# Low rank products of 64 rows in groups of four, first loads in single rows, and later first weight sums in a two-stage LoRA kernel

## The chip, the cores and the metric

The kernel runs on one core of one Trainium2 chip. The metric is the time of one execution on the device in microseconds (us). Lower is better.

## The reference

There are 8 batch elements of 512 tokens and 2048 features, all in 32-bit floats. Two linear layers follow each other, each with its input added. The first picks one of 8 full weights per batch element. The second has one weight, a bias, and a low rank part of rank 16 picked per batch element:

```python
w = weight[adapter_ids]                      # L0: 8 x (2048, 2048)
x = x + jnp.einsum('bsi,boi->bso', x, w)
base_out = jnp.einsum('bti,oi->bto', x, W) + b
lora_h = jnp.einsum('bti,bir->btr', x, A)    # A = lora_As[adapter_mapping]
lora_out = jnp.einsum('btr,bro->bto', lora_h, Bm)
x = x + base_out + lora_out * 2.0
```

## The kernel before

Every product runs on TensorE as 128 x 128 weights against 128 rows by 512 tokens, and each operand is split into a high part (rounded to TensorE's 32-bit format, by ScalarE) and a low part (the rest, a subtraction on VectorE or GpSimd). A full product is then three: high times high, high times low, low times high (L856 to L858 in stage 1).

**Stage 1** (to about 1460 us) computes x1 = x + first layer. It runs over 8 batch elements and 16 output tiles each (128 tiles n). A tile has 16 rows k of 128 inputs, so 48 products, into one of two banks `sums`. VectorE adds x to it (L777) and splits it, and `add_h` (L845, L846) multiplies x1 by A of the low rank part into `h_sum`. `a_mix` holds A four times beside itself (high and low), so that the 128 rows of `h_mix` are four groups of 32; `b_mix` holds B of rank 16 eight times, the last 64 rows as low part. h and B go to DRAM (`hs`, `bs`) for stage 2. In between, VectorE forms sums of blocks of the second weight (`sum_q`, 28 units of four steps, one step per tile), which GpSimd stores (`store_q`).

**The start.** SyncE issues the loads of x (8 pieces `x_first` of 2 rows, 512 KB) and of the first two tiles' weights (8 pieces `W_FIRST` of 4 rows, 256 KB) in a written order. ScalarE (`x_hi_part`, `w_hi_part`) and VectorE (`x_lo_part`, `w_lo_part`) split them in the same order. TensorE does 14 products with zeros meanwhile (L867), then the first two tiles alternately by piece.

**Stage 2** computes the second layer by two nested levels of a fast block scheme: 98 steps s, that is 14 outer (`o` = 0 to 6, twice) with 7 inner ones (`j` = 0 to 6). A step has four tiles m of 12 products (L914). Steps j = 0, 2, 4, 5 write `bank_x`, the others `bank_y`, four banks each. VectorE adds each finished tile to one or two sums in SBUF (L822, L824, `acc_free`), splits the next step's x (`xc_lo`, L751, behind tiles 0 and 1), and forms the one after (`add_terms`, L737 to L744, behind tile 3). Weights come through `wl` (5 buffers), split by ScalarE (L593) and GpSimd (L429).

**Low rank products** (L929). 32 of the 98 steps (table `LOW_RANK`, j = 0, 4 or 5, all with products in `bank_x`) carry four of them. Behind each tile m, one product of 128 rows, `bm` (B) against `hm` (h), goes into `bank_y[m]`, which is idle in such a step. VectorE adds it with the bias behind the additions of the same tile (`add_low_rank`, L701). The next step that writes `bank_y` (j = 1 or 6) waits per tile for that addition, in the line

```python
if j in (1, 6) and before is not None:
    pe.wait_ge(low_rank_added, before + m + 1)
```

SyncE loads `bm` (7 buffers, one per product, L329), each behind the wait for an old product.

Of the kernel before, what the change touches and what calls it, by code (L numbers as in the profile page):

```python
# [5 lines left out]
P = 128  # L6
F32 = mybir.dt.float32
# [64 lines left out]
def build(nc, xT, ids0, ids1, w0T, w1T, bias, lora_a, lora_b, yT):  # L72
# [4 lines left out]
    PARTS = 2  # L77
    NG = P // (2 * R)
    TILES = NB * NT
# [5 lines left out]
    WL = 5  # L85
# [4 lines left out]
    WARM = 14  # L90
# [8 lines left out]
    bs = scratch("bs", (NB, 2, P, HALF * P))  # L99
# [31 lines left out]
    with ExitStack() as ctx:  # L131
# [60 lines left out]
        w_first = [[sem(f"w_first{n}_{part}") for part in range(2 * PARTS)] for n in range(2)]  # L192
# [4 lines left out]
        x_first = [sem(f"x_first{c}") for c in range(XC)]  # L197
# [46 lines left out]
        W_FIRST = [(0, 0), (1, 0), (0, 1), (1, 1), (0, 2), (0, 3), (1, 2), (1, 3)]  # L244

        def w_parts(n):

            return 2 * PARTS if n < 2 else PARTS

        def w_ks(n, part):  # L250
            size = KT // w_parts(n)
            return slice(part * size, (part + 1) * size)

        def w_count(n, part):

            if n < 2:
                return W_FIRST.index((n, part)) + 1
            return len(W_FIRST) + (n - 2) * PARTS + part + 1

        def w_done(n):  # L260

            return w_count(n, w_parts(n) - 1)
# [34 lines left out]
        def _(sp):  # L297
            def load_x_first(c):
                sp.dma_start(x_raw[:, x_rows(0, c)], xT[0, c]).then_inc(x_first[c], 16)  # L299
# [3 lines left out]
            for c in range(2):  # L303
                load_x_first(c)
            sp.wait_ge(ids0_loaded, 16)
            for b in range(NB):
                adapter = sp.value_load(ids_sb[0:1, 0, b:b + 1], min_val=0, max_val=ADAPTERS - 1)
                for t in range(NT):
                    n = b * NT + t
                    s = n % 2  # L310
                    for i, (first_n, part) in enumerate(W_FIRST if n == 0 else ()):
                        ks = w_ks(first_n, part)
                        sp.dma_start(w_raw[first_n][:, ks], w0T[bass.ds(adapter, 1), first_n, :, ks]  # L313
                                     .rearrange("a p k o -> (a p) k o")).then_inc(w_first[first_n][part], 16)
                        for c in ((), (2,), (3,), (), (4, 5), (6, 7), (), ())[i]:
                            load_x_first(c)
                    if n >= 2:
                        sp.wait_ge(w_ready, w_done(n - 2))
                        for part in range(PARTS):
                            ks = w_ks(n, part)  # L320
# [6 lines left out]
            def load_bm(i):  # L327
                b, o = low_rank_place(i)[0:2]
                sp.dma_start(bm[i % BM][:].bitcast(F32), bs[b, o // HALF, :, o % HALF * P:(o % HALF + 1) * P]  # L329
                             ).then_inc(bm_loaded[i % BM], 16)  # L330
# [8 lines left out]
            for s in range(SEQ):  # L339
                for m in range(Q):  # L340
# [4 lines left out]
                    if n == 2 * WL:  # L345
                        sp.wait_ge(b_stored, NB * 2 * 16)
# [23 lines left out]
        def _(pool):  # L370
# [8 lines left out]
            def load_b(b, half):  # L379
                if 2 * b + half > 0:  # L380
                    pool.wait_ge(b_ready, 2 * b + half)
# [51 lines left out]
            pool.wait_ge(x_first[XC - 2], 16)  # L433
# [4 lines left out]
            for b in range(NB):  # L438
                for t in range(NT):
# [26 lines left out]
                    if t == 3 and b < NB - 1:  # L466
                        pool.wait_ge(a_ready, (b + 1) * NG)
# [3 lines left out]
                    if n < UNITS * 4:  # L471
                        u, step = divmod(n, 4)
# [19 lines left out]
            for n in range(3, SEQ * Q + 13):  # L492
# [13 lines left out]
                if n == 17:  # L506

                    pool.wait_ge(h_stored, NB * 16)
                    pool.wait_ge(b_stored, NB * 2 * 16)
# [29 lines left out]
        def _(act):  # L539
            def w_hi_part(n, part):  # L540
# [421 lines left out]
```

## Time and profile before

| | us |
|---|---|
| median of 3 runs | 2564.01 |
| lowest, highest | 2562.82, 3201.55 |
| profiled execution | 2562.13 |
| its span | 2560.6 |
| TensorE busy | 2553.9 |
| VectorE busy | 1666.0 |
| GpSimd busy | 1251.4 |
| ScalarE busy | 875.7 |

Spans and rows are in us from the start of the span of the profiled execution. PE is TensorE, DVE VectorE, ACT ScalarE, POOL GpSimd, SP SyncE; a q behind the name is the engine's queue that issues transfers. A product is drawn with its whole way through the array, so that neighbours overlap; the pace is read from start to start. "Idle before" names who ended the idle time ahead of an instruction.

### The profile page before, as it was taken

The numbers are of one execution on the slowest core, as the hardware profiler recorded it, in microseconds if no ns is written. First come the engines' busy times: TensorE is split into PE (matmuls) and PEld (weight loads), VectorE is DVE, ScalarE is ACT, GpSimd is POOL, SyncE is SP. The second block draws the span as 40 slices with busy tenths as digits, with TensorE's granted clock in tenths as the row PEclk, the third lists the DMA queues.
The fourth block names the chain that finished last, engine by engine and source line by source line (L and its number), as shares of the span: only waits on it lengthen the run. The fifth ranks groups of instructions, "written<-read, shape, count | busy, mean of one in ns | idle before, by whom it ended". The sixth has DMA issues, their size and how long they took to land.

```text
span 2560.6 us, 31029 instructions
## 1 busy us (share of the span) xinstructions
PE 2553.9 (100%) x11246; PEld 2112.2 (82%) x11246; DVE 1666.0 (65%) x1885; ACT 875.7 (34%) x1161; POOL 1251.4 (49%) x1471
## 2 busy tenths in 40 slices
PE   9999999999999999999999999999999999999999
PEld 7888888888888888888888888888888888888887
DVE  5445455454354454364443368999998689999995
ACT  4232232232232232232322234343343343333333
POOL 3434434443454334334323466556666655556655
PEclk9999999999999999999999999999999999999999
DMA  9998888998999887899977887457777855546764
GB/s 340 330 302 295 299 285 282 299 285 281 272 297 336 269 290 273 261 292 284 295 190 196 223 310 265 139 173 251 266 240 254 292 168 175 155 150 203 238 224 143
DMA packets 238939, 648.03 MB, mean 253 GB/s; under 512 B 30148, under 2 KB 46532, under 8 KB 238788
## 3 DMA queue, kind: packets, MB, share of 16 engines
q0 software_dynamic: 123440, 393.28, 48.2%
q1 hardware_dynamic: 115060, 252.24, 30.6%
q8 instruction: 90, 1.47, 0.2%
q14 instruction: 61, 0.50, 0.1%
q10 hardware_dynamic: 288, 0.52, 0.1%
HBM read 433.07 MB, written 212.86 MB: 252 GB/s over the span
## 4 chain that ended last, share of the span: by engine, by line
PE 98%; DMA 1%; SPq 0%; DVE 0%; issue 0%; POOL 0%; POOLq 0%; DVEq 0%
PE bank L914 42%; PE bank L856 18%; PE bank L857 18%; PE bank L858 18%; PE bank L845 1%; PE bank L929 1%; PE bank L846 1%; DMA q_raw<-w1T 1%; DMA ids_sb<-ids 0%; SPq L299 0%; SPq L313 0%; DVE q_raw L712 0%; DVE w_lo L667 0%; POOL q_raw L402 0%; POOLq L375 0%
## 5 line engine op out<-in xcount | busy, mean ns | idle before, releaser
L914 PE MATMUL bank<-xc,wl 128*128 128x512 f32 x4704 | 1087.6, 389 | 0.1
L914 PEld LDWEIGHTS bank<-xc,wl 128*128 128x128 f32 x4704 | 882.9, 188 | 183.7 <-issue 0.5
L856 PE MATMUL bank<-x_hi,w_hi 128*128 128x512 f32 x2048 | 797.1, 389 | 0.9 <-DVE w_lo L667 0.9
L429 POOL TENSOR_TENSOR wl<-wl 128x512 fp32r<-128x512 f32 x392 | 599.5, 1548 | 406.0 <-ACT wl L593 404.4
L857 PE MATMUL bank<-x_lo,w_hi 128*128 128x512 f32 x2048 | 796.8, 389 | 0.0
L858 PE MATMUL bank<-x_hi,w_lo 128*128 128x512 f32 x2048 | 796.7, 389 | 0.0
L547 ACT ACTIVATE w_hi<-w_raw 128x1024 fp32r<-128x1024 f32 (+1 forms) x260 | 258.4, 1039 | 969.5 <-PE bank L858 964.4
L777 DVE TENSOR_TENSOR x_raw<-bank,x_raw 128x512 f32<-128x512 f32 x128 | 88.5, 691 | 693.5 <-PE bank L858 634.5
L856 PEld LDWEIGHTS bank<-x_hi,w_hi 128*128 128x128 f32 x2048 | 384.4, 188 | 82.1 <-DVE w_lo L667 2.0
L858 PEld LDWEIGHTS bank<-x_hi,w_lo 128*128 128x128 f32 x2048 | 384.4, 188 | 79.9
L857 PEld LDWEIGHTS bank<-x_lo,w_hi 128*128 128x128 f32 x2048 | 384.4, 188 | 79.7
L446 POOL DMA_DIRECT2D x1s<-x_raw x128 | 70.1, 548 | 656.1 <-DVE x_raw L777 656.1
L822 DVE TENSOR_TENSOR c<-bank,c 128x512 f32<-128x512 f32 x448 | 295.6, 681 | 102.2 <-PE bank L914 98.7
L593 ACT ACTIVATE wl<-wl 128x512 fp32r<-128x512 f32 x392 | 240.5, 624 | 349.5 <-DMA wl<-w1s 332.8
L751 DVE TENSOR_TENSOR xc<-xq,xc 128x1024 fp32r<-128x1024 f32 x196 | 335.9, 1714 | 5.2 <-ACT xc L604 5.1
L667 DVE TENSOR_TENSOR w_lo<-w_raw,w_hi 128x1024 fp32r<-128x1024 f32 (+1 forms) x260 | 302.6, 1204 | 48.4 <-ACT w_hi L547 48.4
L604 ACT ACTIVATE xc<-xq 128x1024 fp32r<-128x1024 f32 x196 | 206.4, 1054 | 314.9 <-DVE xq L741 133.7
L409 POOL DMA_DIRECT2D w1s<-q_raw x196 | 108.7, 574 | 150.4 <-DVE q_raw L712 62.5
L824 DVE TENSOR_TENSOR c<-c,bank 128x512 f32<-128x512 f32 x224 | 146.6, 676 | 15.9 <-PE bank L914 15.9
L701 DVE SCALAR_TENSOR_TENSOR c<-bank,bias_sb,c 128x512 f32<-128x512 f32 x128 | 96.1, 751 | 4.5
L782 DVE TENSOR_TENSOR x_lo<-x_raw,x_hi 128x512 fp32r<-128x512 f32 x128 | 87.4, 683 | 1.5 <-ACT x_hi L584 1.5
L584 ACT ACTIVATE x_hi<-x_raw 128x512 fp32r<-128x512 f32 x128 | 78.7, 615 | 26.6 <-PE bank L858 17.7
(44 smaller groups left out, 1262.8 us busy)
## 6 DMA issues: line engine op xcount, KB each, us to landing
w_raw<-w0T SPq DMA_DIRECT2D x252, 512.0 KB, 7.7
wl<-w1s SPq DMA_DIRECT2D x392, 256.0 KB, 2.9
xss<-x_raw POOLq DMA_DIRECT2D x256, 256.0 KB, 4.5
w1s<-q_raw POOLq DMA_DIRECT2D x196, 256.0 KB, 7.3
q_raw<-w1T POOLq DMA_DIRECT2D x96, 512.0 KB, 9.8
xq<-xss POOLq DMA_DIRECT2D x40, 1024.0 KB, 6.9
x1s<-x_raw POOLq DMA_DIRECT2D x128, 256.0 KB, 2.9
c<-x1s POOLq DMA_DIRECT2D x32, 1024.0 KB, 7.0
```

The lines of the kernel that those rows point to most:

```text
L429: pool.tensor_tensor(w[:, 1], w[:, 1].bitcast(F32), w[:, 0].bitcast(F32), ALU.subtract).then_inc(wl_ready, 1)
L547: act.activation(w_hi[s][:, ks], w_raw[s][:, ks], ACT.Copy).then_inc(w_hi_done, 1)
L593: act.activation(wl[n % WL][:, 0], wl[n % WL][:, 1].bitcast(F32), ACT.Copy).then_inc(wl_hi_done, 1)
L604: act.activation(xc[s % 2][:, 0, ks], xq[place][:, ks], ACT.Copy).then_inc(xc_hi_done, 1)
L667: dve.tensor_tensor(w_lo[s][:, ks], w_raw[s][:, ks], w_hi[s][:, ks].bitcast(F32), ALU.subtract).then_inc(w_ready, 1)
L751: dve.tensor_tensor(xc[s % 2][:, 1, ks], xq[PLACE[s % INNER]][:, ks], xc[s % 2][:, 0, ks].bitcast(F32), ALU.subtract).then_inc(xc_ready, 1)
L822: op = dve.tensor_tensor(tile, bank[m][:], tile, ALU.add)
L824: op = dve.tensor_tensor(tile, tile, bank[m][:], ALU.subtract)
L856: pe.matmul(sums[s][:], w_hi[s][:, k, :], x_hi[:, k, :], start=(k == 0), stop=False)
L857: pe.matmul(sums[s][:], w_hi[s][:, k, :], x_lo[:, k, :], start=False, stop=False)
L858: mm = pe.matmul(sums[s][:], w_lo[s][:, k, :], x_hi[:, k, :], start=False, stop=(k == KT - 1))
L914: mm = pe.matmul(bank[m][:], w[:, w_part, k, :], x[:, x_part, k, :], start=(p == 0 and k == 0 and BEGIN[j]), stop=(p == 2 and k == Q - 1), ...
```

## The change

- *Shape of the low rank products.* `a_mix` and `b_mix` are laid out so that 64 rows hold all terms (in each half: the high h with low B, the low A's h with high B, the low h with high B, high with high), and the same in the other 64. `bs` is stored in pairs of output tiles; one `bm` of 128 rows holds two tiles' B, 64 rows each. A product reads one half of `bm` and of `hm`.
- *Their place.* All four products of a step stand behind tile m = 2, in the order of halves 0, 1, 0, 1. They wait for all additions of the step before, or, in j = 5 behind j = 4, for all its low rank additions. VectorE adds products 0 and 1 behind the additions of tile 2, and 2 and 3 behind those of tile 3. The waits in j = 1 and 6 stay as they are.
- *Loads of `bm`* go out once per group, two pairs at a time.
- *The start.* The first four rows of x are loaded and split singly, the first weights in pieces of 2, 2 and then 4 rows, in the order of `X_WITH` and `W_FIRST`; for the first four rows TensorE does, per piece of two rows, first high times high, then high times low, then low times high (`add_high_first`). `WARM` is 9 instead of 14.
- *First weight sums.* Unit 0's step 0 stands at tile 2 and its steps 1 to 3 at tile 3 (`q_steps`); all later units stay.

```diff
     NG = P // (2 * R)
+    A_HI = NG + NG // 2
+    ROWS = P // 2
-    WARM = 14
+    WARM = 9
-    bs = scratch("bs", (NB, 2, P, HALF * P))
+    bs = scratch("bs", (NB, 2, HALF // 2, P, P))
...
-        W_FIRST = [(0, 0), (1, 0), (0, 1), (1, 1), (0, 2), (0, 3), (1, 2), (1, 3)]
+        W_FIRST = [(0, 0, 2), (1, 0, 2), (0, 2, 4), (1, 2, 4), (0, 4, 8), (1, 4, 8), (0, 8, 12), (0, 12, 16),
+                   (1, 8, 12), (1, 12, 16)]
+        X_FIRST = [(k, k + 1) for k in range(2 * KX)] + [(c * KX, (c + 1) * KX) for c in range(2, XC)]
+        X_WITH = [(0, 1, 2), (), (3,), (), (4,), (), (5,), (6, 7), (8, 9), ()]
...
+        def q_steps(n):
+            if n < 4:
+                return ((), (), (0,), (1, 2, 3))[n]
+            return (n % 4,) if n < UNITS * 4 else ()
...
                     old = low_rank_tile((n - WL) // Q) if n >= WL else None
-                    if old is not None:
-                        i = old + (n - WL) % Q
+                    if old is not None and (n - WL) % Q == 2:
+                        i = old + Q - 1
                         sp.wait_ge(low_rank_done, i + 1)
-                        if i + BM < 2 * LOW:
-                            load_bm(i + BM)
+                        for pair in (i // 2 - 1, i // 2):
+                            if pair + BM < LOW:
+                                load_bm(pair + BM)
...
             def store_b(b, half):
-                pool.wait_ge(b_ready, 2 * b + half + 1)
-                pool.dma_start(bs[b, half], b_mix[:].bitcast(F32)).then_inc(b_stored, 16)
+                pool.wait_ge(b_ready, (2 * b + half + 1) * 2)
+                for i in range(2):
+                    rows = slice(i * ROWS, (i + 1) * ROWS)
+                    pool.dma_start(bs[b, half, :, rows].rearrange("q p n -> p q n"),
+                                   b_mix[rows, :].bitcast(F32).rearrange("p (q i n) -> p q i n", i=2, n=P)[:, :, i]
+                                   ).then_inc(b_stored, 16)
...
                 for g in range(NG):
                     act.activation(a_mix[:, :, g, 0:R], a_raw[:], ACT.Copy).then_inc(a_hi_done, 1)
+                for g in range(1, NG, 2):
+                    act.activation(a_mix[:, :, g, R:2 * R], a_raw[:], ACT.Copy).then_inc(a_hi_done, 1)
...
-                for g in range(NG):
-                    dve.wait_ge(a_hi_done, b * NG + g + 1)
+                dve.wait_ge(a_hi_done, (b + 1) * A_HI)
+                for g in range(0, NG, 2):
...
             def b_lo(b, half):
                 dve.wait_ge(b_hi_done, 2 * b + half + 1)
-                dve.scalar_tensor_tensor(out=b_mix[P // 2:P, :], in0=b_raw[P // 2:P, :], scalar=LORA_SCALING,
+                for first in range(0, P, ROWS):
+                    rows = slice(first, first + R)
+                    dve.scalar_tensor_tensor(out=b_mix[rows, :], in0=b_raw[rows, :], scalar=LORA_SCALING,
...
-                    if first_low is not None:
+                    if first_low is not None and m >= 2:
                         dve.wait_ge(acc_free, s * Q + m + 1)
-                        add_low_rank(first_low + m, bank_y[m])
+                        for place in ((0, 1), (2, 3))[m - 2]:
+                            add_low_rank(first_low + place, bank_y[place])
...
+            def add_high_first(n, c):
+                rows = range(c * KX, (c + 1) * KX)
+                pe.wait_ge(w_hi_done, w_count(n, rows[0]))
+                for k in rows:
+                    pe.wait_ge(x_hi_done, x_count(0, k))
+                    pe.matmul(sums[n][:], w_hi[n][:, k, :], x_hi[:, k, :], start=(k == 0), stop=False)
+                for k in rows:
+                    pe.wait_ge(x_ready, x_count(0, k))
+                    pe.matmul(sums[n][:], w_hi[n][:, k, :], x_lo[:, k, :], start=False, stop=False)
+                pe.wait_ge(w_ready, w_count(n, rows[0]))
+                for k in rows:
+                    pe.matmul(sums[n][:], w_lo[n][:, k, :], x_hi[:, k, :], start=False, stop=False)
...
-                    if first_low is not None:
-
-                        i = first_low + m
+                    if first_low is not None and m == 2:
+
+                        i = first_low
                         if j == 5 and before is not None:
-                            pe.wait_ge(low_rank_added, before + m + 1)
+                            pe.wait_ge(low_rank_added, before + Q)
                         elif s > 0:
-                            pe.wait_ge(acc_free, (s - 1) * Q + m + 1)
+                            pe.wait_ge(acc_free, s * Q)
                         pe.wait_ge(hm_loaded[i // NT % 2], (i // NT // 2 + 1) * 16)
-                        pe.wait_ge(bm_loaded[i % BM], (i // BM + 1) * 16)
-                        pe.matmul(bank_y[m][:], bm[i % BM][:], hm[i // NT % 2][:], start=True, stop=True
-                                  ).then_inc(low_rank_done, 1)
+                        for place in range(Q):
+                            pair = (i + place) // 2
+                            rows = slice(place % 2 * ROWS, (place % 2 + 1) * ROWS)
+                            pe.wait_ge(bm_loaded[pair % BM], (pair // BM + 1) * 16)
+                            pe.matmul(bank_y[place][:], bm[pair % BM][rows], hm[i // NT % 2][rows],
+                                      start=True, stop=True).then_inc(low_rank_done, 1)
```

## Rows read from the trace of the kernel before

**Rows 1.** Waits of TensorE: who waited for whom, us in total, times, longest.
```profile
PE bank L867 <- DVE x_lo L754: 2.1, 1, 2.1
PE bank L856 <- DVE w_lo L667: 0.9, 2, 0.6
PE bank L845 <- DVE x_lo L782: 0.2, 1, 0.2
```

**Rows 2.** Groups by line: engine, operation, tiles, shapes, count | busy us, mean ns | idle before.
```profile
L914 PE MATMUL bank<-xc,wl 128*128 128x512 f32 x4704 | 1087.6, 389 | 0.1
...
L856 PE MATMUL bank<-x_hi,w_hi 128*128 128x512 f32 x2048 | 797.1, 389 | 0.9 <-DVE w_lo L667 0.9
```

**Rows 3.** Instructions of line 929: duration ns min/median/max, first and last start us.
```profile
L929 PEld LDWEIGHTS bank<-hm,bm x128: 187/188/188, 1507.6 to 2491.5; 128*128 128x128 f32 x128
L929 PE MATMUL bank<-hm,bm x128: 389/389/390, 1507.8 to 2491.7; 128*128 128x512 f32 x128
```

**Rows 4.** Timeline of TensorE at the start: start us, us, line, tiles [idle before].
```profile
2.13 6.34 PE L867 MATMUL bank<-x_lo 128*128 128x512 f32 x14 [2.13 <-DVE x_lo L754]
9.10 0.50 PE L856 MATMUL bank<-x_hi,w_hi 128*128 128x512 f32 x1 [0.64 <-DVE w_lo L667]
9.44 0.40 PE L857 MATMUL bank<-x_lo,w_hi 128*128 128x512 f32 x1
...
11.03 0.50 PE L856 MATMUL bank<-x_hi,w_hi 128*128 128x512 f32 x1 [0.26 <-DVE w_lo L667]
```

**Rows 5.** Timeline of ScalarE at the start, the first weights' high part.
```profile
7.69 0.63 ACT L547 ACTIVATE w_hi<-w_raw 128x512 fp32r<-128x512 f32 x1 [1.63 <-DMA w_raw<-w0T]
```

**Rows 6.** Timeline of TensorE in step j = 5 of the outer step at 1843 us.
```profile
1834.20 0.39 PE L929 MATMUL bank<-hm,bm 128*128 128x512 f32 x1
...
1837.15 0.39 PE L929 MATMUL bank<-hm,bm 128*128 128x512 f32 x1
...
1843.04 0.39 PE L929 MATMUL bank<-hm,bm 128*128 128x512 f32 x1
```

**Rows 7.** Timeline of VectorE in that step and the one before it.
```profile
1828.47 4.05 DVE L751 TENSOR_TENSOR xc<-xq,xc 128x1024 fp32r<-128x1024 f32 x1
...
1842.94 0.69 DVE L824 TENSOR_TENSOR c<-c,bank 128x512 f32<-128x512 f32 x1
...
1844.26 0.75 DVE L701 SCALAR_TENSOR_TENSOR c<-bank,bias_sb,c 128x512 f32<-128x512 f32 x1
1844.93 0.68 DVE L824 TENSOR_TENSOR c<-c,bank 128x512 f32<-128x512 f32 x1
```

**Rows 8.** Timeline of VectorE in the step j = 5 that ends at 2154 us.
```profile
2148.60 4.11 DVE L751 TENSOR_TENSOR xc<-xq,xc 128x1024 fp32r<-128x1024 f32 x1
...
2157.06 0.75 DVE L701 SCALAR_TENSOR_TENSOR c<-bank,bias_sb,c 128x512 f32<-128x512 f32 x1
```

**Rows 9.** Timeline of TensorE there, the first product of the step j = 6.
```profile
2154.27 4.01 PE L914 MATMUL bank<-xc,wl 128*128 128x512 f32 x17
```

**Rows 10.** Timeline of GpSimd beside the split of 1828.47.
```profile
1826.84 2.54 POOL L429 TENSOR_TENSOR wl<-wl 128x512 fp32r<-128x512 f32 x2
1829.32 0.77 POOL L531 DMA_DIRECT2D yT<-c  x1
1830.12 1.30 POOL L429 TENSOR_TENSOR wl<-wl 128x512 fp32r<-128x512 f32 x1
```

**Rows 11.** Groups by line of the page: the splits of xc on VectorE.
```profile
L751 DVE TENSOR_TENSOR xc<-xq,xc 128x1024 fp32r<-128x1024 f32 x196 | 335.9, 1714 | 5.2 <-ACT xc L604 5.1
```

**Rows 12.** Transfers from 0 to 40 us, GB/s per us.
```profile
GB/s 0 0 94 262 418 383 279 195 348 404 414 404 414 422 414 416 424 408 399 176 30 0 78 307 340 389 336 373 258 270 360 414 410 418 422 397 393 401 414 426
```

**Rows 13.** Stretch table of TensorE: us, busy (count), granted clock, DMA share, GB/s.
```profile
4.00:6.00 2.00, 2.00 (x6) 1.00 1.00 400
```

**Rows 14.** DMA issues of the page: count, KB each, us to landing.
```profile
wl<-w1s SPq DMA_DIRECT2D x392, 256.0 KB, 2.9
...
q_raw<-w1T POOLq DMA_DIRECT2D x96, 512.0 KB, 9.8
```

More of the change, by code:

```diff
@@ L191, in build @@
         w_loaded = [[sem(f"w_loaded{s}_{part}") for part in range(PARTS)] for s in range(2)]
-        w_first = [[sem(f"w_first{n}_{part}") for part in range(2 * PARTS)] for n in range(2)]
+        w_first = [sem(f"w_first{i}") for i in range(10)]
         zeros_ready = sem("zeros_ready")
@@ L196, in build @@
         w_ready = sem("w_ready")
-        x_first = [sem(f"x_first{c}") for c in range(XC)]
+        x_first = [sem(f"x_first{i}") for i in range(XC + KX)]
         x_loaded = [sem(f"x_loaded{c}") for c in range(XC)]
@@ L297, in _, with load_x_first @@
         def _(sp):
-            def load_x_first(c):
-                sp.dma_start(x_raw[:, x_rows(0, c)], xT[0, c]).then_inc(x_first[c], 16)
+            def load_x_first(i):
+                first, last = X_FIRST[i]
+                place = x_rows(0, first // KX).start + first % KX
+                rows = xT[0, first // KX][:, first % KX:first % KX + last - first]
+                sp.dma_start(x_raw[:, place:place + last - first], rows).then_inc(x_first[i], 16)
             sp.dma_start(ids_sb[:, 0, :], ids0).then_inc(ids0_loaded, 16)
-            for c in range(2):
-                load_x_first(c)
+            for i in X_WITH[0]:
+                load_x_first(i)
             sp.wait_ge(ids0_loaded, 16)
@@ L310, in _ @@
                     s = n % 2
[L311 to L316, printed above, removed]
+                    for i, (tile, first, last) in enumerate(W_FIRST if n == 0 else ()):
+                        if i > 0:
+                            for piece_x in X_WITH[i]:
+                                load_x_first(piece_x)
+                        sp.dma_start(w_raw[tile][:, first:last], w0T[bass.ds(adapter, 1), tile, :, first:last]
+                                     .rearrange("a p k o -> (a p) k o")).then_inc(w_first[i], 16)
                     if n >= 2:
                         sp.wait_ge(w_ready, w_done(n - 2))
-                        for part in range(PARTS):
-                            ks = w_ks(n, part)
+                        for part, (first, last) in enumerate(w_pieces(n)):
+                            ks = slice(first, last)
                             sp.dma_start(w_raw[s][:, ks], w0T[bass.ds(adapter, 1), t, :, ks]
@@ L470, in _ @@
                         store_h(b - 1)
-                    if n < UNITS * 4:
-                        u, step = divmod(n, 4)
+                    for step in q_steps(n):
+                        u = n // 4
                         store_q(u, step)
@@ L624, in _ @@
                     if n + 2 < TILES:
-                        for part in range(PARTS):
-                            w_hi_part(n + 2, part)
+                        for rows in w_pieces(n + 2):
+                            w_hi_part(n + 2, *rows)
                     x1_hi_part(n)
@@ L778, in _ @@
                     if n + 2 < TILES:
-                        for part in range(PARTS):
-                            w_lo_part(n + 2, part)
+                        for rows in w_pieces(n + 2):
+                            w_lo_part(n + 2, *rows)
                     dve.wait_ge(x1_hi_done, n + 1)
@@ L791, in _ @@
                         b_lo(b, t // 8)
[L792 to L793 removed]
+                    for step in q_steps(n):
+                        sum_q(n // 4, step)
                     if n == TILES - 4:
```

126 lines of the change are left out of this document (64 added, 62 removed).

## The prediction

> **What bounds the kernel now.** I read the waits of TensorE first, because nothing else can set the end if they are short: they total 3.2 us, of which 2.1 us is the start and 0.9 us two waits for the first weights [rows 1]. Then the groups by line: three families of products of stage 1 (L856 stands for them), the products of stage 2 (L914) and three small families of 128 (the low rank ones, L929, stand for them), each with idle time near nothing [rows 2, 3]. The timeline gives the step from one product's start to the next: twelve products and one low rank product take 2.95 us (1834.20 to 1837.15), so 0.227 us each, although each is drawn 0.39 us long, because they overlap [rows 6]. So TensorE is full from 9.10 us to its last product, and only three things can move the time: fewer or cheaper products, an earlier first product, or a new wait of TensorE. The reader is to see one more thing in [rows 6, 7]: VectorE in stage 2 has no idle time in the stretches that hold the low rank products; it runs up to several us behind TensorE and catches up later. That is free today, since nothing of TensorE waits for it [rows 1]. It is what the change leans on.
>
> **The change part by part.** The profiled execution took 2562.13 us for a span of 2560.6 us; the sum is made on it. The median of the runs shown is 2564.01, 1.9 us more.
>
> *Low rank products on TensorE.* Before, 128 products of 128 rows follow one tile each, and cost 128 x 0.227 = 29.1 us, 0.91 us per group of four (32 groups) [rows 3, 6]. After, the four of a group stand together; they read rows 0 to 63, 64 to 127, 0 to 63, 64 to 127 and write four different banks. A product streams 512 columns whatever its rows, so alone a 64-row product costs 0.227 us like the others, and four cost 0.91 us: gain nothing. If the two of a pair run side by side on the two halves of the array, four cost 2 x 0.227 = 0.45 us, the lower bound. No row shows such a pair. The upper bound: if going from full-height to half-height products and back lets the array run empty, each of the two changes costs what lies between a product's length and its step, 0.39 - 0.227 = 0.16 us, and a weight load in the open, 0.19 us [rows 3]: four serial products then cost 0.91 + 2 x 0.35 = 1.61 us. The nearest row for a restart is the first product after a pause: 9.10 to 9.44, 0.34 us, which is 0.11 us over the step [rows 4]. I take pairs side by side and one such restart: 0.57 us. That is 32 x (0.91 - 0.57) = 10.9 us gained; the bounds are 14.5 us gained and 22 us lost.
>
> The Trainium skill's page "TensorE: Matmul & The Clock Gate" (Part 3: Packing small matmuls) says that products at different row positions run concurrently, and has 3.07 times for four of 32 rows; no row here shows it, and by it the pairs would be near the lower bound. Against that stands the Trainium skill's page "TensorEngine Tiling (Array Packing)" (Key Properties): "Mode switching requires drain"; by it the group costs nearer to 1.15 than to 0.57 us. No row of before shows such a switch.
>
> *The additions behind them, on VectorE.* Each low rank product has one addition (L701, 0.75 us drawn, 0.67 us to the next instruction); a tile's own two additions take 1.32 us up to it [rows 7]. Before, the first of a group is done behind the first tile (m = 0). After, the first two stand behind the third tile's additions and the other two behind the fourth's. Their number is the same, but TensorE's next step may not write the first of these banks until its addition is done (the waits in steps j = 1 and 6, which the diff leaves alone). Steps j = 0 and 5 of the groups feed them: 22 such hand-overs. Worked for the one at 1843 us: the third tile's low rank addition starts at 1844.26 behind its own additions; VectorE had no gap, so with two low rank additions (2 x 0.67) gone from in front the same additions end at 1842.92, and the first low rank addition ends 0.70 later, at 1843.62. TensorE would start the next step at 1843.04 + 0.23 = 1843.27 at the old cost [rows 6, 7]: a wait of 0.35 us, where before that bank had been free for almost two tiles. The same subtraction at the largest, 2154 us: 2157.06 - 1.34 + 0.70 = 2156.42 against 2154.27, a wait of 2.15 us [rows 8, 9]. Over all 22 (the low rank products, of which every fourth closes a hand-over, lie from 1507.8 to 2491.7 [rows 3]) nine come out above zero, together 8.6 us, at the old cost of the products. And where TensorE saves, it only arrives earlier: with 0.34 us less per group, and two groups in a row before a step j = 6, twelve of them wait, 14 us in all.
>
> What makes VectorE late there are stretched splits of xc (L751): 1.71 us in the mean, but 4.11 and 4.05 us at some places [rows 7, 8, 11]. At the second, GpSimd works in the same time, subtractions and transfers back to back [rows 10]. The change moves these splits forward by one or two additions. If they then fall beside the same work of GpSimd and end no earlier, the two additions that were hidden in front come on top: 1.34 us more at the ten hand-overs behind two groups, 26 us in all. If they fall into its gaps and all have their mean of 1.71 us [rows 11], VectorE needs 1.3 + 1.7 = 3.0 us per tile in the first two tiles of such a step, 0.3 over the 2.72 of TensorE, and the waits shrink to under 0.4 us each, about 4 us in all. I take 12 us, nearer the row-by-row sum.
>
> *The start.* Before, the first real product waits for w_hi and w_lo of four rows, whose weights land behind two pieces of x of 512 KB: ScalarE starts on them at 7.69, VectorE behind it, TensorE at 9.10 [rows 4, 5]. After, three rows of x (768 KB) and two rows of weights (128 KB) stand there instead of 1024 and 256 KB: 384 KB less, at about 400 GB/s in this stretch [rows 12] 0.96 us. ScalarE's part is half the columns of the instruction of 0.63 us and some fixed share, about 0.4 us, and the first product (high times high) needs no lower part, so it starts at about 7.69 - 0.96 + 0.4 + 0.05 = 7.2 us: 1.9 us earlier. The pause of 0.26 us before 11.03 goes too, with its restart, 0.4 us together [rows 4]. Against it: the 14 warm-up products ran one every 0.43 us (2.13 to 8.46), the pace of 1.2 GHz, and the real ones at 9.10 at the 2.4 GHz pace; the granted clock is given as 1.00 even there, so only the pace tells [rows 4, 13]. With 9 warm-ups and products from 7.2 us, some three would still run at the slow pace until 8.5: 0.6 us lost. Sum: 1.7 us gained. Bounds: 2.3 us gained if no real product is slow; 0.5 us lost if a dozen real products run at the slow pace (12 x 0.2 = 2.4 us), as TensorE now pauses between 6 and 7 us, where it did not. After that data keep up: 6 MB (4 of x, 2 of weights) at 400 GB/s need 15 us, TensorE needs 96 x 0.227 = 21.8 us for the same rows. VectorE has as much to do as before.
>
> *At no cost.* The first weight sums come at tiles 2 and 3 instead of 0 to 3. TensorE needs nothing of them before stage 2, and each tile of stage 1 lasts 48 x 0.227 = 10.9 us, so that a wait of VectorE or ScalarE of under 10 us is covered. What is late next: unit 1's four loads of 512 KB go out behind tile 3 and are wanted behind tile 4, 10.9 us later, against a landing time of 9.8 us [rows 14]. Were it to slip, VectorE has until the end of the next tile. Two more short copies of A on ScalarE and two fewer subtractions on VectorE per batch, one more VectorE instruction per half of B: same cover. GpSimd issues 16 more stores of b, spread over stage 1, with no waiter before stage 2. SyncE issues 64 loads of bm instead of 128. Its wait for a group's last product stands between the transfers of wl for two tiles; it lasts no longer than the group does, under 1 us, and wl lands 2.9 us after its issue, five tiles (13.6 us) ahead of its use [rows 14]. Without that lead it would cost the 1 us, 32 times.
>
> **Sum:** 2562.13 - 10.9 + 12 - 1.7 = 2561.5; with the 1.9 us to the median 2563.4, so 2563 us.
>
> **The rivals.**
> *A, the gain holds:* pairs side by side, stretched splits fall into gaps, 4 us of waits: 2564 - 12.5 (at 0.52 us per group) - 2 + 4 = 2553 us. For it: the splits' stretch depends on what GpSimd does at that moment [rows 10]. Against: in 9 of 22 places VectorE is late already at the old cost.
> *B, slower than before, through VectorE:* splits that end no earlier, 26 us of waits with the products at 0.57: 2564 - 10.9 + 26 - 1.7 = 2577 us. It decides once the waits pass 12.6 us. For it: [rows 7, 8, 10]. Against: it needs the same bad meeting ten times.
> *C, no side by side:* serial products with a run-empty at each change, 1.61 us: + 22 us, and as TensorE comes later, waits of only 3 us: 2587 us. In a plain serial case (0.91 us) it is 2564 + 8.6 - 1.7 = 2571 us. For it: no row shows a pair. Pairs side by side with the array run empty twice cost 0.45 + 0.7 = 1.15 us, + 7.8 us, waits 6 us: 2576 us. This last form is what the Trainium skill's sentence on the drain ("TensorEngine Tiling (Array Packing)", Key Properties) makes of it.
>
> **How the numbers follow.** Forecast (its own range 2558 to 2568): 0.35. A: 0.32. B: 0.13. C in its three forms: 0.20. From 2549 us (A with the lower bound of the products and nearly no waits) to 2580 us (B, and C but for its worst) leaves out about 0.15. Two per cent is 51 us, about what a measurement of this kernel can tell from no change: none of the cases reaches it. Faster 0.01, same 0.97, slower 0.02.
>
> **What would show it.** The four low rank products start within 0.5 us as two pairs (steps of under 0.05 and of 0.23 us) or not; TensorE's waits list one for VectorE at the additions with bias, in steps j = 6 and 1, of 12 us in all, the longest 2 to 3 us near 2150 and 2330 us; the first real product stands at 7.2 us. I am wrong if the waits are near zero with pairs side by side (A), or if the low rank group costs over 1 us.

## The result, and the profile after

| | before | after |
|---|---|---|
| median, us | 2563.41 (6 runs) | 2575.53 (6 runs) |
| ratio, 95% interval | | 1.0051 (1.004 to 1.0061) |
| profiled span, us | 2560.6 | 2574.3 |
| TensorE busy, us | 2553.9 | 2557.0 |

The change makes the kernel 12 us slower, 0.5%. That is under 2%, but clear of zero. (One of the six executions of the kernel before took 3201.55 us; without it their median is 2562.82 us.) First the waits of TensorE after, in the form of [rows 1] (who waited for whom, us in total, times, longest):

```profile
PE bank L964 <- DVE c L855: 5.4, 4, 2.0
PE bank L964 <- DVE c L857: 3.9, 2, 2.3
PE bank L914 <- DVE x_lo L792: 2.1, 1, 2.1
PE bank L889 <- DVE w_lo L696: 1.2, 1, 1.2
PE bank L903 <- ACT w_hi L575: 0.5, 1, 0.5
```

The first two rows are new, 9.3 us: in stage 2 TensorE now waits for VectorE. The list names the additions of products (L855, L857); the addition with bias, L739, is what the code waits for at that place. Of the waits in stage 2 that are over 0.25 us, every one but one stands at the first product of a step j = 6. The largest, in the timelines of TensorE and VectorE after (compare [rows 8, 9]):

```profile
2155.35 0.73 PE L982 MATMUL bank<-hm,bm 64*128 64x512 f32 x4
2156.01 3.02 PE L964 MATMUL bank<-xc,wl 128*128 128x512 f32 x12
2161.07 4.11 PE L964 MATMUL bank<-xc,wl 128*128 128x512 f32 x10 [2.04 <-DVE c L855]
```
```profile
2153.73 2.92 DVE L789 TENSOR_TENSOR xc<-xq,xc 128x1024 fp32r<-128x1024 f32 x1
2156.57 1.27 DVE L855 TENSOR_TENSOR c<-bank,c 128x512 f32<-128x512 f32 x2
2157.77 1.21 DVE L789 TENSOR_TENSOR xc<-xq,xc 128x1024 fp32r<-128x1024 f32 x1
2158.90 1.28 DVE L855 TENSOR_TENSOR c<-bank,c 128x512 f32<-128x512 f32 x2
2160.22 1.41 DVE L739 SCALAR_TENSOR_TENSOR c<-bank,bias_sb,c 128x512 f32<-128x512 f32 x2
```

The third tile's products ended at 2155.4, but VectorE reaches their additions only at 2158.90, and the first low rank addition starts at 2160.22 and ends some 0.7 us later; TensorE, free since 2159.0, goes on at 2161.07. The stretch table of TensorE (us, busy and count, granted clock, DMA share, GB/s) shows what came next:

```profile
2158.00:2160.90 2.90, 1.03 (x5) 1.00 0.87 268
2161.90:2164.40 2.50, 2.50 (x7) 0.50 0.47 49
2165.00:2170.00 5.00, 5.00 (x23) 1.00 0.65 236
```

After the wait, TensorE ran at half its clock (0.50, 1.2 GHz) for 3.4 us: from product to product it took 0.427 us instead of 0.227. The longest wait of this execution, 2.3 us before 2244.1 us, had no such stretch behind it.

The group of four low rank products, in the two rows of its line (compare [rows 3]):

```profile
L982 PEld LDWEIGHTS bank<-hm,bm x128: 182/184/186, 1513.3 to 2502.3; 64*128 64x128 f32 x128
L982 PE MATMUL bank<-hm,bm x128: 392/443/493, 1513.3 to 2502.5; 64*128 64x512 f32 x128
```

The rows give the length of one instruction; the price of a group is read from start to start. The two products of a pair start 3 ns apart: they do run side by side. But from the last full product to the first pair are 0.32 us, from pair to pair 0.33, from the second pair to the next full product 0.32, and from that to the one after 0.34, where each step between full products is 0.227 us. These distances are the same in all 32 groups to within 1 ns (the group at 2155 us above: 0.66 us from its first product to the next full one). A group costs 0.318 + 0.335 + 0.325 + 0.338 - 2 x 0.227 = 0.86 us, and six slightly longer steps behind it 0.03 more: 0.89 us, against 0.91 before.

The start after, in the timeline of TensorE (compare [rows 4]) and in the table by stretch, before and after (in the latter the columns are TensorE, its weight loads, VectorE, ScalarE, GpSimd, granted clock, DMA share, GB/s):

```profile
6.85 1.22 PE L903 MATMUL bank<-x_hi,w_hi 128*128 128x512 f32 x2 [0.52 <-ACT w_hi L575]
...
13.85 0.61 PE L909 MATMUL bank<-x_hi,w_lo 128*128 128x512 f32 x2
15.66 0.50 PE L889 MATMUL bank<-x_hi,w_hi 128*128 128x512 f32 x1 [1.20 <-DVE w_lo L696]
```
```profile
9.00:12.00 3.00, 2.64 (x10) 1.90 (x11) 1.51 (x3) 2.39 (x3) 0.00 (x0) 1.00 1.03 407
```
```profile
9.00:12.00 3.00, 3.00 (x10) 2.33 (x10) 1.36 (x3) 1.12 (x3) 0.00 (x0) 1.00 0.85 284
```

The first real product starts 2.25 us earlier, but the transfers move less in the stretch from 9 to 12 us (284 GB/s, the last row, against 407 before), the first real products run at the slow pace until about 10.9 us (two take 0.85 us), and the piece with x's fifth row is late: ScalarE starts to split it at 12.7 us, before at about 11.1, and TensorE goes on at 15.66 behind the splits of it and of its weights. The first addition of A's product (L845 before, L879 after) starts 0.56 us later than before, the third one and all later ones to the end of stage 1 within 0.02 us of before. So in this execution the start brings nothing, and all 13.7 us of the span come in stage 2. That varies from execution to execution: the first product of stage 2 stands at 1461.1 us here and in the kernel before, and at 1459.9 and 1461.8 us in early and early_again (below), which have the stage 1 of after.

### The profile page after: what moved, and what is told of

The parts are those of the page before. It is cut to its first block, busy times and chain, and to the rows that moved or that the text cites. A ratio compares the mean times of both kernels' runs of the same rounds, so it can differ in the third digit from the quotient of the medians.

```text
span 2574.3 us, 30906 instructions
## 1 busy us (share of the span) xinstructions
PE 2557.0 (99%) x11241; PEld 2095.2 (81%) x11241; DVE 1682.2 (65%) x1889; ACT 882.7 (34%) x1181; POOL 1267.4 (49%) x1487
## 4 chain that ended last, share of the span: by engine, by line
PE 96%; DVE 1%; DMA 1%; issue 1%; SPq 0%; POOL 0%; ACT 0%; POOLq 0%; DVEq 0%; ACTq 0%
PE bank L964 39%; PE bank L891 18%; PE bank L889 18%; PE bank L890 18%; PE bank L879 1%; PE bank L880 1%; PE bank L982 1%; DVE c L855 1%; DVE xc L789 0%; DMA ids_sb<-ids 0%; DMA xq<-xss 0%; DMA wl<-w1s 0%; SPq L321 0%; DVE c L857 0%; SPq L337 0%
## 5 line engine op out<-in xcount | busy, mean ns | idle before, releaser
L457 POOL TENSOR_TENSOR wl<-wl 128x512 fp32r<-128x512 f32 x392 | 601.9, 1554 | 420.7 <-ACT wl L627 418.8
L575 ACT ACTIVATE w_hi<-w_raw 128x1024 fp32r<-128x1024 f32 (+2 forms) x262 | 258.7, 1033 | 965.3 <-PE bank L891 963.2
L855 DVE TENSOR_TENSOR c<-bank,c 128x512 f32<-128x512 f32 x448 | 296.2, 683 | 112.3 <-PE bank L964 108.2
L789 DVE TENSOR_TENSOR xc<-xq,xc 128x1024 fp32r<-128x1024 f32 x196 | 342.5, 1748 | 8.9 <-ACT xc L638 8.7
L696 DVE TENSOR_TENSOR w_lo<-w_raw,w_hi 128x1024 fp32r<-128x1024 f32 (+2 forms) x262 | 303.1, 1198 | 47.8 <-ACT w_hi L575 47.7
L857 DVE TENSOR_TENSOR c<-c,bank 128x512 f32<-128x512 f32 x224 | 146.7, 678 | 16.3 <-PE bank L964 16.1
L739 DVE SCALAR_TENSOR_TENSOR c<-bank,bias_sb,c 128x512 f32<-128x512 f32 x128 | 90.2, 747 | 2.3
L478 POOL DMA_DIRECT2D xss<-x_raw x96 | 87.4, 1027 | 0.3
```

The lines of the kernel that those rows point to most:

```text
L457: pool.tensor_tensor(w[:, 1], w[:, 1].bitcast(F32), w[:, 0].bitcast(F32), ALU.subtract).then_inc(wl_ready, 1)
L575: act.activation(w_hi[s][:, ks], w_raw[s][:, ks], ACT.Copy).then_inc(w_hi_done, 1)
L696: dve.tensor_tensor(w_lo[s][:, ks], w_raw[s][:, ks], w_hi[s][:, ks].bitcast(F32), ALU.subtract).then_inc(w_ready, 1)
L789: dve.tensor_tensor(xc[s % 2][:, 1, ks], xq[PLACE[s % INNER]][:, ks], xc[s % 2][:, 0, ks].bitcast(F32), ALU.subtract).then_inc(xc_ready, 1)
L855: op = dve.tensor_tensor(tile, bank[m][:], tile, ALU.add)
L857: op = dve.tensor_tensor(tile, tile, bank[m][:], ALU.subtract)
```

## The experiments

Theory H: the loss is the hand-over at the steps j = 6, made by the later additions. Theory D: the loss is the change of the array's height. All edits are to the kernel after, or to the one before where it says so. Times are medians; the kernel before ran beside each, at 2563.5 to 2563.7 us.

**early.** Products behind the second tile, additions two, one, one.

```diff
-                    if first_low is not None and m >= 2:
+                    if first_low is not None and m >= 1:
...
-                        for place in ((0, 1), (2, 3))[m - 2]:
+                        for place in ((0, 1), (2,), (3,))[m - 1]:
...
-                    if first_low is not None and m == 2:
+                    if first_low is not None and m == 1:
```

> The kernel after, with the four low rank products behind the second tile of a step instead of the third, and their additions spread: two behind the second tile, one each behind the third and fourth. Theory H (the loss is TensorE's wait at the start of the steps j = 6, because the first addition of the group comes behind the third tile's): the first addition now ends about 2.7 us before TensorE needs the bank, so the waits of 9.3 us and the slow stretch of 1.8 us behind the one at 2158 us go, and the time is about 2562 to 2564 us, level with the kernel before. Theory D (the rival: what costs is the change between 128-row and 64-row products, and the group itself): the number of changes is the same, so the time stays at 2573 to 2577 us.

Measured: 2561.08 us, ratio 0.9991 (0.9982 to 1.0001), 0.9 us under the range expected by theory H. The loss is gone whole. Its waits of TensorE are these two rows and no more, both at the start:

```profile
PE bank L914 <- DVE x_lo L792: 2.1, 1, 2.1
PE bank L903 <- ACT w_hi L575: 0.6, 1, 0.6
```

The step at 2150 us in its timeline of VectorE:

```profile
2147.51 1.28 DVE L855 TENSOR_TENSOR c<-bank,c 128x512 f32<-128x512 f32 x2
2148.83 1.41 DVE L739 SCALAR_TENSOR_TENSOR c<-bank,bias_sb,c 128x512 f32<-128x512 f32 x2
```

The first low rank additions stand one tile earlier than in the kernel after and are done at 2150.2 us, 2.6 us before the next step starts (2152.8). The group costs the same as after (0.86 us), so theory D can't explain the 14 us between the two.

**adds_late.** Only the products moved: `m == 1` for them on TensorE, the additions left where the kernel after has them.

> The kernel after, with the four products of 64 rows behind the second tile, but the additions where the kernel after has them (two behind the third tile, two behind the fourth). It parts the place of the products from the place of the additions. Theory H (the additions' place makes the hand-over waits): the waits stay, 2572 to 2577 us. Rival (the products' place does: low rank products that come late make VectorE wait): 2561 to 2563 us, as with both moved.

Measured: 2575.46 us, ratio 1.0059 (1.0037 to 1.0081). Its waits of TensorE in stage 2:

```profile
PE bank L964 <- DVE c L855: 4.6, 3, 2.3
PE bank L964 <- DVE c L857: 3.9, 2, 2.0
PE bank L964 <- issue: 0.8, 2, 0.4
```

So it is the place of the additions, not that of the products. The granted clock stayed at 1.00 in its profiled execution, and the loss is the same as after within the intervals; the slow stretch of 1.7 us is a smaller part of the loss after.

**place_only.** The kernel before, with four full products behind the third tile, additions two and two, and the loads of bm issued four at a time.

```diff
...
-                        if i + BM < 2 * LOW:
-                            load_bm(i + BM)
+                        for k in range(old, old + Q):
+                            if k + BM < 2 * LOW:
+                                load_bm(k + BM)
...
+                        for place in range(Q):
+                            one = i + place
+                            pe.wait_ge(bm_loaded[one % BM], (one // BM + 1) * 16)
+                            pe.matmul(bank_y[place][:], bm[one % BM][:], hm[i // NT % 2][:], start=True, stop=True
+                                      ).then_inc(low_rank_done, 1)
```

> The kernel before, with only the place changed: four full products of 128 rows together behind the third tile, the additions two and two behind tiles three and four. No product of 64 rows, no change of the array's height. Theory H: the hand-over waits are there all the same, 8 to 11 us, and a slow stretch if one of them is over 2 us: 2571 to 2575 us. Theory D: no change of height, no loss: 2562 to 2565 us.

Measured: 2580.71 us, ratio 1.0059 (1.0042 to 1.0076), 5.7 us above the range expected by theory H. With no change of height at all the loss is there. Every step into, inside and out of a group is 0.227 us here, so what these steps cost more in the kernel after comes with the 64 rows, not with four products standing together. The profiled execution (2584.96 us, the slowest of its four) waits 10.9 us for VectorE in six places, and has three slow stretches, some 5 us of loss together, each behind one of its three longest waits. Its waits, and the stretch table of TensorE:

```profile
PE bank L916 <- DVE c L823: 5.5, 3, 2.3
PE bank L916 <- DVE c L825: 5.4, 3, 2.2
```
```profile
1613.30:1616.60 3.30, 3.30 (x10) 0.51 0.49 107
1695.30:1698.50 3.20, 3.18 (x8) 0.50 0.32 44
2255.00:2258.30 3.30, 3.30 (x10) 0.52 0.60 187
```

It is not a clean half of the change: the 7 buffers of bm hold 7 tiles' B here and 14 in the kernel after, and TensorE also waits 1.3 us for ScalarE's part of the second weights once.

**rows64_single.** The kernel before, with products of 64 rows, one behind each tile, additions as before. The layout of A, B and h that 64 rows need, and loads of bm as pairs, come with it.

```diff
...
-                        pe.wait_ge(bm_loaded[i % BM], (i // BM + 1) * 16)
-                        pe.matmul(bank_y[m][:], bm[i % BM][:], hm[i // NT % 2][:], start=True, stop=True
+                        pair = i // 2
+                        rows = slice(i % 2 * ROWS, (i % 2 + 1) * ROWS)
+                        pe.wait_ge(bm_loaded[pair % BM], (pair // BM + 1) * 16)
+                        pe.matmul(bank_y[m][:], bm[pair % BM][rows], hm[i // NT % 2][rows],
...
```

> The kernel before, with only the shape changed: 64-row products, one behind each tile as before, additions as before. Each of the 128 stands between full products, so it pays two changes of height and has no partner. In the trace of the kernel after, the group of four costs 0.88 us over full products without it, of which two pair steps of 0.33 us at most; the two changes then are some 0.3 us. Theory D and H agree here that a lone product costs 0.227 + 0.3 = 0.5 to 0.6 us, 128 x 0.3 = 35 to 40 us more: 2598 to 2606 us. If changes of height are free it stays at 2563 us, and the 0.88 us must come from something else.

Measured: 2618.4 us, ratio 1.0215 (1.0198 to 1.0232), 55 us over before and 12 us above the range expected. TensorE's timeline, two low rank products with twelve full ones between:

```profile
1522.16 0.50 PE L943 MATMUL bank<-hm,bm 64*128 64x512 f32 x1
1522.58 2.99 PE L926 MATMUL bank<-xc,wl 128*128 128x512 f32 x12
1525.50 0.49 PE L943 MATMUL bank<-hm,bm 64*128 64x512 f32 x1
```

From 1522.16 to 1525.50 are 3.34 us, against 2.95 before [rows 6]. From start to start, in the median of the 128, there are 0.318 us into the low rank product, 0.425 out of it, 0.337 for the next step and some 0.02 more behind it: 0.42 us over four steps of 0.227, and 128 x 0.42 = 54 us. So for a lone product the two changes of height cost 0.42 us together. A group of four pays them once, and less: of the distances in the kernel after, those into and out of the group are 0.33 us over the usual step (the steps behind it included), and the one from pair to pair 0.11. Together they eat the 0.45 us that the two pairs save.

**after_small_pool.** The kernel after, with GpSimd's subtraction of the low part cut to a quarter of its columns; three quarters of these low parts are left as they were loaded.

```diff
-                pool.tensor_tensor(w[:, 1], w[:, 1].bitcast(F32), w[:, 0].bitcast(F32), ALU.subtract
+                pool.tensor_tensor(w[:, 1, 0:1], w[:, 1, 0:1].bitcast(F32), w[:, 0, 0:1].bitcast(F32), ALU.subtract
```

> The kernel after, but GpSimd's subtraction for the low part of the second weights covers only the first of four row blocks of each tile (it leaves out three quarters of that work, so these low parts are wrong). It tests whether VectorE is late because its splits of xc are stretched while GpSimd works. Theory: with GpSimd's 1.55 us cut to about 0.5 us, the splits fall from 1.75 us in the mean to 1.3 us, and the hand-over waits of 9.3 us shrink to 0 to 2 us: 2561 to 2564 us. Rival (VectorE is late by its own work or by late loads): splits and waits stay, 2573 to 2577 us.

Measured: 2560.63 us, ratio 0.9989 (0.998 to 0.9999). It has no wait of TensorE in stage 2. Splits of xc (L789) and GpSimd's subtractions (L457) by line, first two rows the kernel after, last two this run (compare [rows 11]):

```profile
L789 DVE TENSOR_TENSOR xc<-xq,xc 128x1024 fp32r<-128x1024 f32 x196 | 342.5, 1748 | 8.9 <-ACT xc L638 8.7
L457 POOL TENSOR_TENSOR wl<-wl 128x512 fp32r<-128x512 f32 x392 | 601.9, 1554 | 420.7 <-ACT wl L627 418.8
L789 DVE TENSOR_TENSOR xc<-xq,xc 128x1024 fp32r<-128x1024 f32 x196 | 241.1, 1231 | 4.3 <-ACT xc L638 4.2
L457 POOL TENSOR_TENSOR wl<-wl 128x128 fp32r<-128x128 f32 x392 | 225.0, 583 | 779.0 <-ACT wl L627 777.2
```

The splits take 1.23 us each (1.69 at most), where they took 1.75 in the kernel after (6.0 at most); VectorE's additions are unchanged (L855: 0.69 us, 0.68 after). With that VectorE is in time, and the late additions cost nothing. So both are needed for the loss: additions behind the third tile, and splits stretched by GpSimd's work.

**early_rows128.** The kernel before with full products behind the second tile, the additions two, one, one, and the loads of bm as in place_only.

> The kernel before, with four full products of 128 rows together behind the second tile and their additions spread two, one, one; nothing of 64 rows, the old start and the old weight sums. It gives what the 64-row shape is worth at the good place: a group of four costs 0.91 us here and 0.88 us with pairs, so the two differ by 32 x 0.03 = 1 us. Expected 2562.5 to 2564 us with no hand-over wait. If the change of height cost more than the trace shows, this would be clearly below 2561 us.

Measured: 2567.47 us, ratio 1.0015 (1.0005 to 1.0024), 3.5 us above the range expected. It has no change of height. Its low rank products wait for the loads of B:

```profile
  DMA bm<-bs: 5.8, 10
```

That is what the weight loads and products of line 933 waited, in us and times, both counted; from product to product the five late ones add 2.7 us. Its profile has a slow stretch at the start as well (9.20 to 12.50 us at a clock of 0.51). The trace divides the loss: stage 2 takes 4.3 us longer than in the kernel before, 2.7 of them at these products, and it starts 0.8 us later, behind a stage 1 that has the slow stretch. So the 64-row shape seems worth some us here in another way than meant, since one buffer holds two tiles' B; that more buffers would cure this run was not tried.

**The start and the sums.** start_only is the kernel before with the new start; q_only, with the new place of the first weight sums; early_old_start, "early" with the old start; early_warm14, "early" with 14 warm-ups (`WARM = 14`); early_w4, "early" with the weights in pieces of four rows:

```diff
...
-        W_FIRST = [(0, 0, 2), (1, 0, 2), (0, 2, 4), (1, 2, 4), (0, 4, 8), (1, 4, 8), (0, 8, 12), (0, 12, 16),
-                   (1, 8, 12), (1, 12, 16)]
+        W_FIRST = [(0, 0, 4), (1, 0, 4), (0, 4, 8), (1, 4, 8), (0, 8, 12), (0, 12, 16), (1, 8, 12), (1, 12, 16)]
...
-        X_WITH = [(0, 1, 2), (), (3,), (), (4,), (), (5,), (6, 7), (8, 9), ()]
+        X_WITH = [(0, 1, 2), (3,), (4,), (5,), (6, 7), (8, 9), (), ()]
```

> The kernel before, with only the new start: single rows of x first, weights in pieces of 2, 2 and 4 rows, 9 warm-ups, high times high first. The trace of the kernel after starts its first real product 2.3 us earlier (6.85 us) and ends the first two tiles 0.5 us later. If the start gives nothing, as that says, the time is 2563 to 2564 us; if the gain was lost only to the weight sums that moved, it is 2561 to 2562 us.

> The kernel before, with only the first weight sums at tiles 2 and 3. In the trace of before, the sum of unit 0 holds VectorE until 40.2 us and the second tile's x1 is late by 0.5 us at 43.8 us. Expected: that 0.5 us goes, 2562.9 to 2563.2 us; by the rival (new waits for unit 1's loads) 2565 us or more.

> Products and additions as in the run with both behind the second tile (2561.1 us), weight sums as after, but the start of before (pieces of two rows of x, four of weights, 14 warm-ups). The start alone measured 2562.7 against 2563.5 us. If the new start is worth its 0.8 us, this is 2561.8 to 2562.5 us; if the start is worth nothing, 2561 us.

> The run with both behind the second tile, with 14 warm-up products instead of 9. The fast pace came at 8.3 us in the trace of before (14 warm-ups without a pause) and at 11.6 us with 9 warm-ups and a pause. With 14 the warm-ups end at about 8.5 us, 1.5 us behind the first real product's data. If the pause is what keeps the slow pace, the first twelve real products run at 0.227 instead of 0.427 us from 8.6 us on: 2560 to 2561 us, no loss by the later start. If the pace has nothing to do with it, the start is 1.6 us later and so is the end: 2562.5 us.

> The run with both behind the second tile, with the first weights in pieces of four rows again (256 KB, 2 KB per partition) and x in single rows. In the trace of after, the transfers move 224 GB/s from 6 to 9 us and 284 from 9 to 12, against 274 and 407 before; the weight pieces of 1 KB per partition are the suspect. Expected: 350 GB/s or more from 9 to 12 us, the pieces of x from the fifth row on land 1 to 2 us earlier, and the time is 2559.5 to 2561 us. If the single rows of x are the cause, the rate stays under 300 GB/s and the time at 2561 to 2562.5 us.

| run | median, us | ratio, 95% interval |
|---|---|---|
| start_only | 2562.74 | 0.9995 (0.9986 to 1.0005) |
| q_only | 2563.25 | 0.9998 (0.9989 to 1.0008) |
| early_old_start | 2562.35 | 0.9997 (0.9987 to 1.0006) |
| early_warm14 | 2561.5 | 0.9994 (0.9985 to 1.0004) |
| early_w4 | 2567.59 | 1.0011 (1.0002 to 1.002) |

The first four can't be told from the kernel before, nor from each other. By the medians the start and the weight sums are worth 1.1 us together; the interval of start_only alone allows a gain of up to 3.6 us. In early_warm14 the fast pace came at 7.7 us and all real products ran at it, from 7.9 us on. It won nothing: TensorE then waited until 15.3 us for the piece with x's fifth row, where after went on at 15.7. So the slow pace did not bound the start there; that late piece did. early_w4 moves more in the first stretch, as was expected (385 GB/s from 9 to 12 us), and is still slower. Its waits say why:

```profile
PE bank L878 <- DVE a_mix L714: 5.7, 1, 5.7
PE bank L902 <- ACT w_hi L574: 2.9, 2, 2.2
```

The second row is the first piece of weights, which now lands later (first product at 8.55 us, in "early" at 6.98). The first row is the split of A, which TensorE awaits at 32 us. A itself had landed at 25 us; ScalarE's copies of it were queued behind the weights of the third tile, in ScalarE's timeline:

```profile
31.30 1.06 ACT L574 ACTIVATE w_hi<-w_raw 128x1024 fp32r<-128x1024 f32 x1 [7.89 <-DMA w_raw<-w0T]
```

Why these weights landed so late was not tried. A slow stretch of 3.4 us (clock 0.50, from 37.6 us) comes with that wait. This run doesn't tell what faster first transfers are worth alone: the wait near 15 us is gone, and the last product of the first two tiles starts at 31.9 us as after, though the first one came 1.7 us later, but the third tile's weights undo it.

**early_again.** The same kernel as early, in more rounds.

> The kernel after with products and additions behind the second tile once more, in more rounds, to see whether it beats the kernel before. The first time gave 2561.1 against 2563.5 us, a ratio of 0.9991 with an interval up to 1.0001. Its trace saves 0.03 us at each of 32 groups and has no hand-over wait, and its start and weight sums measured 0.8 and 0.3 us alone. Expected by these terms: 1 to 2.5 us under before, ratio 0.9990 to 0.9996, the interval about 0.0007 wide to either side.

Measured: 2562.46 us, ratio 0.9995 (0.9986 to 1.0004). Twice a little under before, and neither time clear of it: the best version found is level with the kernel before. The same kernel can differ by a slow stretch: this profiled execution has one (3.4 us at 0.50, from 16.2 us, behind a wait of 2.6 us), the one of early has none, and their spans are 2560.8 and 2558.5 us.

## Why the prediction was wrong

The forecast was 2563 us, no change; measured 2575.5. The time lies in the range, near rival B's 2577 us and the 2576 us of C's last form, but not by their ways: B had the group at 0.57 us and 26 us of waits, C's form 1.15 and 6, and measured were 0.89 and 12.5. Step by step:

- *What bounds the kernel, and what the change leans on:* right. VectorE's lead was the cover of the low rank additions, and the change used it up.
- *The hand-over waits, 12 us:* right in mechanism, and in size partly by luck. In the trace the distances above 0.24 us between products of stage 2, outside the groups and the slow stretch, add up to 12.5 us over the step; the list of waits has 9.3 of them. The 12 us were drawn from a sum of 14 that counted on TensorE saving 0.34 us per group, which it did not. At the group's true cost, the row-by-row subtraction had 8.6 to 9 us, so it was some 30% short. The places were partly wrong. The eight large waits stand at j = 6 in the outer steps 1 to 4 of both groups. Five of these (1685, 1764, 1843, 2154, 2391 us in the time of before) had come out above zero in the subtraction; three, of 1.2 to 2.5 us, had come out at nothing or below; and the 2.1 us forecast near 2335 us, at j = 1, did not come. Which split is stretched changes when the order does. after_small_pool shows that the stretch is GpSimd's, which the prediction could only suppose; adds_late and early show that the additions' place makes it count.
- *The price of a group, 0.57 us taken:* this is the step that failed. Measured 0.89 us. The pairs are side by side, as taken, but both changes of height are paid (0.33 us over the usual steps), and the second pair comes 0.33 us after the first, not 0.227: its weight loads start 0.11 us behind the first pair's products, where a load between full products starts 3 ns behind. The prediction took one restart of 0.11 us for all of it; its own case with two run-empty changes, 1.15 us, was about as far off on the other side. That a 64-row product alone costs 0.227 us like the others failed too: between full products it costs 0.64 us. The term was 10.9 us and measured 32 x 0.02 = 0.6 us. The Trainium skill's page "TensorEngine Tiling (Array Packing)" (Key Properties) states "Mode switching requires drain". The trace agrees that a switch costs time (0.32 us on either side of a group; the first 64-row weight load starts 0.317 us behind the last full product, not 3 ns), and rows64_single gives the price for a lone product, 0.42 us there and back. The same page (Theoretical Speedup) has "Up to 2×" for 64 rows; here a pair that follows a pair takes 0.33 us where two full products take 0.45, a factor of 1.4, and with the switches the group of four gains 2%.
- *The start, 1.7 us taken:* nothing by the landmarks in stage 1 of this profile, and by the medians of the runs 0.8 us, not clear of zero. The first product was placed well (7.2, measured 6.85). Missed were the slow pace, which lasted to about 10.9 us rather than 8.5, and the late piece with the fifth row of x; by early_warm14 it is the second that bounds the start. The bound given (0.5 us lost) held.
- *No cost for the weight sums, A and B:* nothing speaks against it. q_only measured no difference; A and B were not run alone, but early, which has them, is level with before.
- *A slow stretch behind a long wait:* not in the forecast. It cost 1.7 us in the profiled execution of the kernel after; other executions need not have it.

With the measured prices the same sum is 2562.13 - 0.6 + 12.5 + 1.7 = 2575.7 us for the profiled execution, which took 2575.93. The error of the forecast on that basis (2575.9 against 2561.5) is 14.4 us: the group 10.3, the start 1.7, the slow stretch 1.7 and the waits 0.5, with 0.2 left over.

## What to carry to other kernels

An engine that is never waited for can still be at its limit for stretches: before a result of it is asked for later, compare, at each place where its result is handed over, when it starts there and when the other side would go on. Two half-height products side by side save at best one product, but going to them and back cost 1.4 to 1.9 products' time here, and a second pair behind the first saved only half a product (0.335 us against 0.454). By these figures, an estimate that no run tested, each further pair in a group would gain 0.12 us, so they pay only when many stand together. Where a change has one gain and one delay, price the gain with its entry and exit: that was 10.3 of the 14.4 us of error here.

## What was not expected of the hardware

- VectorE's split of 128x1024 from SBUF takes 1.23 us when GpSimd's subtraction beside it is cut to 0.58 us, and 1.75 us in the mean, up to 6.0 us, when it is 1.55 us long. VectorE's additions that read a bank take 0.68 to 0.69 us either way.
- In five of the fourteen profiled executions TensorE's granted clock was 0.50 (1.2 GHz) for stretches of 3.4 us: at 2161 us in the kernel after, three times in place_only, and in the first 40 us of early_rows128, early_w4 and early_again. Each began during a wait of 2.0 to 5.7 us or up to 1.4 us after TensorE went on. Other waits of the same length had none: 2.3 us in the kernel after (before 2244 us) and 2.3 us in adds_late. What decides between them stayed open.
- A pair of 64-row products on different halves starts 3 ns apart; a single one between full products costs 0.64 us instead of 0.227.
